# A two-layer graph network: VectorE halves the products of the last four tiles of a group before TensorE sums them

## The reference, cut to what matters

```
h = sqrt(2) * relu(emb @ W1 / sqrt(10))            # (E, 16)
w = (h @ W2 / sqrt(16)).reshape(E, 7, 16, 8)       # weights of each edge
s_out, g_out, v_out = einsums of the edge's node features with w
edge_ftr = concat([1.593*tanh(s_out), 1.593*tanh(g_out) * v_out]) * norm
out = segment_sum(edge_ftr, edge_dst)
```

## Time and profile before

| What | Value |
|---|---|
| Median of 3 runs | 1520.99 us (1516.53 to 1529.5) |
| The profiled execution: its own time | 1531.05 us |
| Its span, first to last instruction | 1528.7 us |
| Mean granted TensorE clock | 0.701 of full speed |
| TensorE matmuls busy | 784.7 us, 51% |
| VectorE busy | 926.1 us, 61% |
| ScalarE busy | 674.3 us, 44% |
| GpSimd busy | 824.9 us, 54% |
| 24 stretches with gathers, 94.01 to 706.40 us | 612.39 us |
| The 3 stretches after them, 706.40 to 771.10 us | 64.70 us |

### The profile page before, as it was taken

How to read it: one execution, slowest core, us unless ns; L and a number is a source line. 1 busy time by engine, 2 the same in 40 slices (tenths; PEclk the granted TensorE clock), 3 DMA queues, 4 the chain that set the end, 5 groups by cost and what they waited for, 6 DMA issues and landing times.

```text
span 1528.7 us, 15502 instructions
## 1 busy us (share of the span) xinstructions
PE 784.7 (51%) x4772; PEld 626.0 (41%) x4772; DVE 926.1 (61%) x1689; ACT 674.3 (44%) x1671; POOL 824.9 (54%) x795
## 2 busy tenths in 40 slices
PE   0066676666766676767764133435343369970000
PEld 0055555555555555555652022212221169960000
DVE  4266676666666665667735877557587889970000
ACT  0056565656565656566634336546451122210000
POOL 6545555555555455552008886637470038877775
PEclk9987978797879787978875565656555555555555
DMA  3111110112111102110027249858673100000000
GB/s 59 36 44 30 34 34 14 30 34 58 19 30 35 33 14 55 34 32 10 23 80 165 33 46 86 54 96 75 75 52 57 30 3 10 9 10 10 10 11 9
DMA packets 40519, 60.36 MB, mean 39 GB/s; under 512 B 17347, under 2 KB 30935, under 8 KB 40182
## 3 DMA queue, kind: packets, MB, share of 16 engines
q0 software_dynamic: 25184, 12.32, 15.6%
q1 hardware_dynamic: 12074, 46.84, 9.3%
q10 hardware_dynamic: 3180, 0.21, 0.2%
HBM read 40.33 MB, written 19.36 MB: 39 GB/s over the span
## 4 chain that ended last, share of the span: by engine, by line
DVE 21%; PE 17%; issue 16%; ACT 13%; POOL 13%; DMA 6%; DVEq 6%; another core or an unknown queue 6%; SPq 0%; POOLq 0%; ACTq 0%
POOL out_dram L623 13%; PE sums L986 10%; DVE h1d_or_products L1317 4%; DMA src_everywhere<-src_by_columns 3%; DVE h1d_or_products L1308 3%; ACT agg_or_stacks L708 2%; ACT agg_or_stacks L717 2%; ACT L738 2%; PE turnB L962 2%; ACT stack_turned L717 2%; DVEq L1307 2%; PE tens L976 2%; DVE dstat L1336 2%; ACT below L816 2%
## 5 line engine op out<-in xcount | busy, mean ns | idle before, releaser
L590 POOL DMA_INDIRECT x_rows<-in_x,src_index x196 | 185.1, 944 | 258.7 <-PE tens L980 218.2
L986 PE MATMUL sums<-h1d_or_products,ident 128*128 128x192 f32 (+1 forms) x1344 | 285.8, 369 | 39.5 <-issue 29.3
L623 POOL DMA_INDIRECT out_dram<-agg_or_stacks,scatter_index x196 | 210.4, 1074 | 161.5 <-DVE agg_or_stacks L1683 99.5
L614 POOL DMA_INDIRECT agg_or_stacks<-run_sums,sum_row_index x196 | 231.4, 1180 | 115.8 <-DVE features_or_scores L1591 57.0
L986 PEld LDWEIGHTS sums<-h1d_or_products,ident 128*128 128x128 f32 x1344 | 249.7, 235 | 61.7 <-issue 44.6
L590 POOL DMA_INDIRECT x_rows<-in_x,dst_index x196 | 193.9, 989 | 64.9 <-issue 64.9
L1317 DVE TENSOR_TENSOR h1d_or_products<-tens,hid 128x768 f32<-128x768 f32 x168 | 156.5, 950 | 104.3 <-PE tens L980 104.3
L1055 PE MATMUL small<-one_column,steps 128*128 128x1 f16 x196 | 38.1, 195 | 167.8 <-DVE steps L1466 70.3
L1055 PEld LDWEIGHTS small<-one_column,steps 128*128 128x128 f16 x196 | 24.7, 126 | 196.5 <-ACT below L816 73.0
L726 ACT ACTIVATE h1d_or_products<-tens,hid 128x48 f32<-128x48 f32 x448 | 87.7, 330 | 0.0
L717 ACT COPY agg_or_stacks<-turnA 96x896 bf16<-96x896 bf16 x42 | 37.9, 902 | 91.8 <-PE turnA L962 46.5
(11 more groups left out here) (273 smaller groups left out, 2162.5 us busy)
## 6 DMA issues: line engine op xcount, KB each, us to landing
src_everywhere<-src_by_columns SPq DMA_DIRECT2D x14, 896.0 KB
xin<-in_x SPq DMA_DIRECT2D x27, 449.5 KB
out_dram<-xin SPq DMA_DIRECT2D x27, 449.5 KB
x_rows<-in_x,src_index POOLq DMA_INDIRECT x196
x_rows<-in_x,dst_index POOLq DMA_INDIRECT x196
run<-run_sums SPq DMA_DIRECT2D x1, 3136.0 KB
agg_or_stacks<-run_sums,sum_row_index POOLq DMA_INDIRECT x196
out_dram<-agg_or_stacks,scatter_index POOLq DMA_INDIRECT x196
```

What stands on the lines that cost most here:

```text
L590: nc.gpsimd.indirect_dma_start(xs[:, t, side, :], None, x, bass.IndirectOffsetOnAxis(ap=idx[:, t:t + 1], axis=0)).then_inc(s_gath[g % LEAD ...
L614: nc.gpsimd.indirect_dma_start(aggr[:, t, :], None, rs, bass.IndirectOffsetOnAxis(ap=ridx[:, t:t + 1], axis=0)).then_inc(s_rsg[g % LEAD2], 16)
L623: nc.gpsimd.indirect_dma_start(out, bass.IndirectOffsetOnAxis(ap=sidx[:, t:t + 1], axis=0), aggr[:, t, :], None, bounds_check=N - 1, oob_i ...
L986: mm = nc.tensor.matmul(sums[:, a * OUTS:b * OUTS].rearrange("p (c o) -> p c o", o=OG), ident[:], prod[:, 2 * a:2 * b, j, :], start=(j == ...
```

## The change

`halve_rest(g)` is new on VectorE: it adds the upper 8 terms of the products of tiles 3 to 6 to the lower 8, 8 x 8 x 24 = 1536 elements a partition, both inputs and the output in SBUF. It stands in the next group between the multiplies of tiles 0 and 1, and once more behind the last group. It waits for ScalarE's tile 3 of the group. TensorE's `sum_rest` then sums 8 terms, 4 in each half, and waits for `halve_rest` in place of the multiplies themselves.

```diff
             def sum_rest(g, half):
                 if half == 0:
-                    pe.wait_ge(s_tfree, (g + 1) * NDV)
-                    pe.wait_ge(s_tact, g + 1)
-                mm = sum_tiles(TACT, GA, half * HID // 2, (half + 1) * HID // 2, HID)
+                    pe.wait_ge(s_half2, g + 1)
+                mm = sum_tiles(TACT, GA, half * HID // 4, (half + 1) * HID // 4, HID // 2)
                 if half == 1:
                     mm.then_inc(s_sumB, 1)
...
+            def halve_rest(g):
+                v.drain()
+                dve.wait_ge(s_tact, g + 1)
+                v.tensor_tensor(prod[:, 2 * TACT:, 0:HID // 2, :], prod[:, 2 * TACT:, 0:HID // 2, :],
+                                prod[:, 2 * TACT:, HID // 2:, :], ALU.add).then_inc(s_half2, 1)
...
                 multiply(g, b, 0)
+                if past(g, 0):
+                    halve_rest(g - 1)
                 multiply(g, b, 1)
...
             group(NP - 1, 1)
+            halve_rest(NG - 1)
             outputs(NG - 1, 1)
             messages(NG - 1, 1)
```

More of the change, by code:

```diff
@@ L364, in build_gnn @@
         s_half = sem("first_tiles_halved")
+        s_half2 = sem("last_tiles_halved")
         s_sumA = sem("first_tiles_summed")
```

## The result

The changed kernel took 1464.07 us (median of 4 runs, 1449.13 to 1472.54) beside 1523.74 us before (1516.53 to 1529.5): ratio 0.958, 95% interval 0.948 to 0.967. The ratio leaves out the changed kernel's slowest run (1472.54 us), which lies over 1.5% above its fastest; the median of the other three is 1459.91 us. The forecast, 1528 us, was wrong; the time is that of the first rival in full (1461 us). The experiments then showed that the gain isn't there in every session on the chips: in the one session in which the kernel before had no late news of TensorE and the changed kernel ran beside it, the change made it 1.5% slower. Late news means here that TensorE has ended its transposes, and that ScalarE, which waits for nothing else, starts its copy only some microseconds later.

What follows compares the result with a forecast made beforehand. Bound taken: a circle through the gather burst and late news of TensorE's chunk 4. 1531.05 + 7.2 (holds) - 0.1 (last groups) = 1538 us, against the median 1528 us; own range 1517 to 1536, wider range 1474 to 1542.

Steps and rivals of the forecast that it cites:

- the first rival: Gather stretches: with 16 fewer TensorE records chunk 4's news comes early; 55 us in B, 5 in A, 1461 us; chance 0.28.
- What bounds the kernel: 24 stretches with gathers, 25.5 us each: TensorE's news arrives late, chunk 4's copy 11.5 us behind the burst's start.
- If chunk 4 is pinned to the burst, finishing earlier buys nothing: TensorE's `sum_rest`: 16 of 32 records removed, 2.7 us a group, lie beside the burst and were costed at nothing.
- The addition: VectorE before `outputs`: 1756 ns for 1536 elements, covered by 2.18 us idle in A, 3.12 in B; costs nothing.
- The holds: GpSimd's bursts: gathers held by the addition end bursts 0.48 us (A) and 1.10 us (B) later; charged 0.3 a stretch, 7.2 us.
- The new wait: TensorE's first half of `sum_rest` starts 1.2 us late, with 1.3 us of work; chunk 4 still ready within the 11.5 us.
- The constancy is the point: ScalarE's copy of chunk 4: comes 11.5 us behind the start of the burst, whatever TensorE had left to do.
- The last groups: Last four groups, without gathers: addition costs 1.8 us, then gains of about 1.0 and 0.9; together -0.1 us.
- The second: Bursts between products of tiles 5 and 2: holds delay chunk 4 in full, 19.0 us slower, 1540 us; chance 0.20.
- the third: TensorE waits for the addition so long that chunk 4 comes behind the 11.5 us; called small, within the rest's 0.06.

Runs made afterwards that it cites:

- e13: Kernel before, switched every four groups: as before, 8 terms, pause, gathers held, as changed, addition with 32 records; 8 terms alone 25.6 us a stretch for 25.5.
- e15: Kernel before, varied every few groups: pause, addition nobody waits for, pause with 8 terms, pause with addition; addition alone 23.35 us a stretch on average, from 25.5.
- e16: Kernel before, only GpSimd's burst of 8 gathers varied every few groups: one break 23.9 us a stretch, two 22.6, small memsets 25.4, as before 25.7.
- e17: Kernel before with a GpSimd memset of 896 elements ahead of the fourth and seventh gather of each burst, from the third group on; 1470.0 us, ratio 0.961.
- e18: As e17, with such a memset also ahead of every third of 42 gathers issued at the start, from the seventh on; 1471.3 us, ratio 0.959.

## Why the prediction was wrong

**What bounds the kernel: right for this kind of session.** Late news of TensorE, only with gathers, worth 81 us in 24 stretches.

**"If chunk 4 is pinned to the burst, finishing earlier buys nothing": right.** 8 terms alone: 25.6 us a stretch (e13), 25.6 with the pause as well (e15). Where nothing is pinned the same 16 records are worth 1.5 us a stretch, the cover's price that I left to the rival.

**The addition: right in size, its cover not.** Forecast 1756 ns and a start 1.9 us behind the multiply; measured 1758 ns (28 of them) and 357.00 - 355.10 = 1.90 us. Its cover was the late news, and went with it: VectorE now has no idle time before `outputs`.

**The holds: right in size, wrong in effect. This is the step that failed, shown in kind B.** I had the fourth gather of B at 0.96 us more than 0.94; it took 1.91. For the fifth of A I had 0.72 us more; in the stretch from 324.34 us it took 1.69. I then asked only whether the late news moves with the end of the burst, and charged 0.3 us a stretch, 7.2 us in all. In B the hold stretched the distance from the fourth gather to the fifth from 1.25 to 2.20 us, and such a break ends the late news (e15), also where only GpSimd makes it, ahead of the fourth, and there in both kinds (e16, e17). In A the hold stretched the one from the fifth to the sixth to 1.99 us, and there the cause stays open: chunk 4 came in time in the changed kernel (9.62 us behind the first gather), but not with the same hold in e15's stretches 10 and 12, nor in e13's 18 and 20, which were built as changed (11.65 and 11.64 us). So the break accounts for the 38.5 us of kind B, and for the 21.4 us of kind A no run separates what did it. The bounds of that term went from nothing to +19 us; a gain wasn't excluded by any row. The earlier trace rows had been read as proof that holds don't matter, since A's two holds left the 11.5 us alone: they are 0.31 and 0.06 us long and fall on the sixth and the eighth gather, too small and too late to tell. The Trainium skill, page "SBUF — State Buffer", calls the port an exclusive lock, and both holds agree with it.

**The new wait: longer than forecast in A.** I had chunk 4 turned by 414.4 us, 7.9 us behind the first gather, with 1.3 us for half of `sum_rest`. In the A stretch from 324.34 us it was turned at 340.08 us, 9.6 us behind it: the 8 records took 2.72 us up to the transposes, since the granted clock was 0.50 there. That is still within the 11.5 us, as I had said.

**"The constancy is the point": overread.** 11.5 us in every row said that the burst sets it, but every burst in the trace had the same unbroken beginning. What a changed burst would do, no row could tell, and the change alters the burst.

**The last groups:** forecast -0.1 us; the three stretches alone cost 2.2 us (66.88 for 64.70), 1.9, 1.2 and -0.9 us one by one. I had worked out 1.8 for the first and -1.0 for the third, and put nothing down for the second.

**The rivals.** The first had the time (1461 us) and, in its main form, the wrong reason: neither fewer records nor the pause cures anything. The Trainium skill's page "NOTIFIC — the notification-queue block", by which fewer records would mean less stall, was cited there; e13's 16 fewer records made no difference (25.6 us for 25.5). The reason stood in the rival's last sentence on B, "a hold that splits the burst", without a test or a share of the chance of its own, and the agreement of the time is luck: its 60 us were 55 from B and 5 from A, and measured are 38.5 and 21.4. The second (+19 us) and the third didn't occur.

## What to carry to other kernels

When a wait is tied to a burst on another engine, ask what the change does to the shape of that burst before costing what it takes away, and let an instruction's lengthening count with either sign. A cover that is itself a stall can go with the change, and the price of what lay under it (here 2.3 us a stretch) is then paid. A gain that rests on a stall should be measured in more than one session: here the same change gave 4.2% and 3.7% in two and took 1.5% in a third.

## What the runs showed of the hardware

- One unchanged kernel took 1410 to 1428 us in three sessions and 1519 to 1533 us in the others, and chip 3 showed both. Durations of single instructions didn't differ (a gather 0.94 us, spaced 1.25, in either); what differed was how late other engines heard of TensorE's work, and of VectorE's own at the start, while gathers ran.
- In late sessions the news stops from about the third or fourth gather of an unbroken row (1.25 us apart) and comes near the row's end, 11.5 us behind the start of 8, and 10.3 us behind the transposes beside a row of 17 (e18). One distance of 1.97 us ahead of the fourth gather, or 2.2 us ahead of the fifth, lets it through; 1.98 us ahead of the sixth alone didn't (e15), nor did 1.33 us each time (e16). In the changed variants of e13, chunk 4 was still late in stretches of kind A, which the whole changed kernel doesn't show; that is unexplained.
- A VectorE addition with both inputs in SBUF held a gather that began 0.68 us behind it: 1.91 us for 0.94. The addition itself took 1758 ns on average over 28, so it wasn't held.
- What holds the news back, whether the recording of the trace has a part in it, and what makes a session late, no run here shows.
